# Attention and expert layer: closing the table of exponent banks, and moving four small operations on a head's maxima one place later

## The reference, cut to what matters

```python
xn = layernorm(x)                                   # x: 2 x 2048 x 256
q, k, v = split(xn @ w_qkv.T)                       # 16 heads of 16 columns
q, k = rope(q), rope(k)
attn = softmax(q @ k.T / 4)                         # per batch and head, 2048 x 2048
s = (attn @ v) @ w_out.T
e = argmax(xn @ gate_w.T)                           # one of 8 experts per token
f = (relu(xn @ wg[e])**2 * (xn @ wu[e])) @ wd[e]
out = x + s * silu(f)
```

## Time and profile before

| | us |
|---|---|
| Three runs: median (lowest to highest) | 1486.63 (1484.91 to 1490.43) |
| The profiled execution: its own time | 1485.04 |
| Its span, from the first to the last instruction | 1483.3 |
| PE busy in the span | 1450.7 (98%) |
| DVE busy | 1346.4 (91%) |
| ACT busy | 1192.4 (80%) |
| Mean granted TensorE clock | 0.998 of full |

### The profile page before, as it was taken

The page is one execution under the profiler, slowest core; times in us unless marked ns, Lnnn a source line. Parts: engine busy times, 40 slices in busy tenths (PEclk is TensorE's granted clock), DMA queues, the critical chain, the costliest instruction groups (busy, mean ns, idle before and its releaser), DMA issues.

```text
span 1483.3 us, 31996 instructions
## 1 busy us (share of the span) xinstructions
PE 1450.7 (98%) x11197; PEld 652.2 (44%) x11197; DVE 1346.4 (91%) x1979; ACT 1192.4 (80%) x2381; POOL 162.1 (11%) x221
## 2 busy tenths in 40 slices
PE   7999999999999999999999999999999999999988
PEld 5555444434475433343434344434444444434326
DVE  6689999999846999999999999999999999999906
ACT  3653588888867888888888888888888888888890
POOL 5433322200001222000010000000010000000110
PEclk9999999999999999999999999999999999999999
DMA  5875244436263455333332342333323433333323
GB/s 186 277 204 137 65 84 83 76 46 125 39 188 90 80 111 99 52 48 48 48 44 41 48 99 42 46 46 48 48 44 45 97 48 41 48 48 48 69 70 117
DMA packets 79801, 119.55 MB, mean 81 GB/s; under 512 B 28962, under 2 KB 66210, under 8 KB 72738
## 3 DMA queue, kind: packets, MB, share of 16 engines
q1 hardware_dynamic: 73714, 105.82, 36.0%
q0 software_dynamic: 3072, 8.39, 2.2%
q10 hardware_dynamic: 2896, 3.62, 0.7%
HBM read 77.15 MB, written 39.71 MB: 79 GB/s over the span
## 4 chain that ended last, share of the span: by engine, by line
PE 94%; ACT 3%; DVE 1%; issue 1%; DMA 1%; SPq 0%; POOL 0%; ACTq 0%; POOLq 0%
PE ps L1243 39%; PE ps L1257 36%; PE ps L1231 5%; PE ps L1159 3%; ACT arena L658 2%; PE ps L1437 2%; PE ps L1160 1%; PE ps L1390 1%; PE ps L1374 1%; PE ps L1192 1%; PE ps L1184 1%; PE ps L1171 1%; PE ps L1341 1%; ACT x_sb L658 1%; PE ps L1136 0%
## 5 line engine op out<-in xcount | busy, mean ns | idle before, releaser
L1231 PE MATMUL ps<-ks,qs 48*128 48x512 f32 x1984 | 692.7, 444 | 0.0
L1243 PE MATMUL ps<-qs,ks 50*128 50x512 f32 x2048 | 680.6, 435 | 9.3 <-ACT x_sb L658 7.6
L809 DVE TENSOR_REDUCE arena<-ps 128x1 f32<-128x512 f32 x992 | 639.0, 681 | 16.5 <-PE ps L1231 16.2
L658 ACT ACTIVATE arena<-ps 128x512 f32<-128x512 f32 x1056 | 564.3, 605 | 86.9 <-PE ps L1243 79.7
L812 DVE TENSOR_REDUCE arena<-ps 128x1 f32<-128x1024 f32 x496 | 603.7, 1217 | 0.8 <-PE ps L1231 0.7
L658 ACT ACTIVATE x_sb<-ps 128x512 f32<-128x512 f32 x992 | 535.3, 598 | 64.9 <-PE ps L1243 44.9
L1243 PEld LDWEIGHTS ps<-qs,ks 50*128 50x128 f32 x2048 | 329.5, 184 | 485.0 <-issue 200.9
L1231 PEld LDWEIGHTS ps<-ks,qs 48*128 48x128 f32 x1984 | 325.2, 184 | 16.5 <-DVE arena L809 9.3
L1257 PE MATMUL ps<-arena 128*32 128x256 f32 (+1 forms) x3104 | 308.5, 469 | 5.5 <-ACT arena L658 4.1
L1257 PE MATMUL ps<-x_sb,arena 128*32 128x256 f32 (+1 forms) x2960 | 290.2, 464 | 0.0
L1257 PEld LDWEIGHTS ps<-arena 128*32 128x32 f32 x3104 | 62.3, 108 | 125.6 <-issue 125.6
(11 more groups left out here) (116 smaller groups left out, 623.2 us busy)
## 6 DMA issues: line engine op xcount, KB each, us to landing
qs<-parts_d SPq DMA_DIRECT2D x186, 128.0 KB
ks<-parts_d SPq DMA_DIRECT2D x186, 128.0 KB
parts_d<-arena SPq DMA_DIRECT2D x64, 256.0 KB, 2.8
xs_d<-arena SPq DMA_DIRECT2D x13, 384.0 KB, 3.5
arena<-xs_d SPq DMA_DIRECT2D x13, 384.0 KB, 3.8
ys_d<-arena SPq DMA_DIRECT2D x13, 384.0 KB, 2.8
x_sb<-in_x SPq DMA_DIRECT2D x2, 2048.0 KB, 13.1
onum_d<-arena SPq DMA_DIRECT2D x124, 32.0 KB
```

The lines of the kernel that those rows point to most:

```text
L658: nc.scalar.activation(prob_of(pi, s, kb)[:, c * W:(c + 1) * W], ps[:, bank, :], ACT.Exp, scale=SCALE).then_inc(exp_done[bank], 1)
L809: nc.vector.tensor_reduce(most[head_slot][:, tile, u:u + 1], ps[:, AB + lo, :], AX.X, ALU.max).then_inc(a_reduced[u], 1)
L1231: ins = nc.tensor.matmul(ps[:, AB + c, :], qs[head_slot][ABASE:ABASE + KR, tile * P:(tile + 1) * P].bitcast(F32R), ks[head_slot][ABASE:ABA ...
L1243: nc.tensor.matmul(ps[:, bank, :], ks[s][at:at + KS, kb * P:(kb + 1) * P].bitcast(F32R), qs[s][at:at + KS, c * W:(c + 1) * W].bitcast(F32R ...
```

## The change

It does two things. The table gets a second bend, at place 89. The swapped order that place 25 brings is turned back there, and the table ends 0 1 2 before it starts 0 1 2 again. An assertion says so. And each k of `cut_maxima` is one place later: a step has two places for these operations, behind u = 0 and behind u = 2. The formula gives k = 0 at kb = 10, u = 2 before the change, and at kb = 11, u = 0 after it. So k = 0, 1, 2, 3 stood at (10, 2), (11, 0), (11, 2), (12, 0), and then stand at (11, 0), (11, 2), (12, 0), (12, 2).

```diff
-        BENDS = (25,)
+        BENDS = (25, 89)
...
         BANKS = banks_of_pair()
+        assert BANKS[:NBB] == [BANKS[(n - NBB) % len(BANKS)] for n in range(NBB)]
...
                     if not last_pair or (s == 0 and ahead < KB):
                         reduce(g + AHEAD, (s + 1 + ahead // KB) % 2, ahead % KB, u)
-                    k = 2 * (ahead - KB) + u // 2 + 1
+                    k = 2 * (ahead - KB) + u // 2
                     if u != 1 and 0 <= k < CUTS and coming:
                         cut_maxima(k, pi * 2 + (s + 1), 1 - s, s, (pi + 1) * 64)
```

## The result

The changed kernel took 1490.76 us in the median (1490.21 to 1491.95, 6 runs), against 1484.87 for the kernel before, measured beside it (1484.17 to 1490.43, 6 runs). The ratio is 1.0034 with a 95% interval of 1.0019 to 1.0050, so the change made the kernel 2.8 to 7.4 us slower. The forecast was 1492.3 us, in a range of 1485 to 1500. The profiled execution has a span of 1489.1 us, 5.8 more than before.

The account below looks back on a forecast made before the run. The prediction took DVE, slower than PE by 0.08 us per two steps, to set the pace. It summed +21.3 - 8.7 - 6.9 = +5.7 us, forecasting 1492.3 us after adding 1.6 for the runs' median, range 1485 to 1500.

Parts of the forecast that it names:

- DVE sets the pace: DVE's back-to-back reductions take 4.65 us per two steps against PE's 4.57, so each DVE instruction counts in full.
- The saving on DVE alone: Reduction of the maxima no longer waits for the reduction right ahead: 0.23 us at 30 heads, 6.9 us gained.
- The rival that PE could not follow: The 0.23 us per head come back as waits for PE: 6.9 us more, 1499.2 us; chance 0.09.
- The wrap: Where pairs meet, place 0 waits for place 126's exponential; closing the table saves DVE 0.62 us 14 times, 8.7 us.
- The new bend: Place 89 repeats place 25 in the other head, behind a 1.0 us product with the values; costed at nothing.
- The shift becomes the late one: B score 0 waits for the later shift transfers: DVE loses 0.76 us at 28 heads, 21.3 us.
- The 0.95 us of slack: Before the change, the last shift lands at 4.05 us behind the transposition, 0.95 us before B score 0 at 5.00.
- 0.4 were named as a sign: Sign in the changed kernel's timeline: a pair takes 0.4 us more than before.
- A transfer's time: Fourth shift transfer, from issue to landing: taken as 1.8 us, between bounds of 1.45 and 1.9.
- The rival with 2.2 us: Shift landing takes 2.2 us, making the wait 1.16 us: 11.2 us more, 1503.5 us; chance 0.05.
- The sum: Whole kernel: shift wait +21.3, wrap -8.7, DVE's own wait -6.9, giving +5.7 us.

Follow-up runs that it names:

- `close_k`: Kernel before with bends at 25 and 89 and the first three operations behind u = 0, 1, 2 of step 11, transposition unmoved: 1467.9 us, ratio 0.9882.
- `bend_80`: Kernel before with the second bend at place 80 instead of 89, the four operations unmoved: 1483.9 us, ratio 1.0001.
- `table_only`: Kernel before with the second bend at place 89 only, the four operations unmoved: 1474.8 us, ratio 0.9932.
- `no_bends`: Kernel before with no bend at all, the four operations unmoved: 1484.8 us, ratio 1.0008.
- `last_12_1b`: `close_k` with only the transposition moved one reduction later, behind u = 1 of kb = 12: 1467.7 us, ratio 0.9903 to the kernel before.
- `last_13_0`: Changed kernel with only the transposition one place later, behind u = 0 of kb = 13: 1562.7 us, ratio 1.0495 to the kernel before.
- `last_12_2b`: `close_k` with only the transposition moved two reductions later, behind u = 2 of kb = 12: 1491.8 us, ratio 1.0067 to the kernel before.
- `move_only`: Kernel before with its own table (bend at 25 alone), the four operations moved as in the change: 1494.3 us, ratio 1.0069.
- `two_more_b`: `close_k` with two more small transfers to memory issued ahead of the four shift transfers: 1471.4 us, ratio 0.9926 to the kernel before.

## Why the prediction was right

**DVE sets the pace.** Right. The saving on DVE alone came back in full in `close_k`: 0.22 us a head against 0.23 forecast. The rival that PE could not follow is out. The Trainium skill (VectorE: DVE Perf Modes, "The DRAIN you can't avoid") says that a semaphore between chained operations costs nothing extra. This case does not bear it out: with one reduction put between the operation and the one it waits for, the head got 0.22 us shorter, and the medians differ by 6.9 us.

**The wrap.** Forecast 14 x 0.62 = 8.7 us, measured 14 x 0.63 = 8.8 by the heads and 9.7 by the medians. The new bend costs nothing, and `bend_80` shows that this hangs on the place: at place 80 it cost what it saved.

**The shift becomes the late one.** Right to its sizes. The landing and the release were put at 4.10 us behind the transposition, and 4.10 was measured. DVE's loss per head was put at 0.76 and is 0.75 where it was read above. By the heads it is 38.50 - 37.70 = 0.80, and the border read above has one of the shorter gaps (0.67 us, where they lie between 0.66 and 0.73 from 685 us on). The forecast had one landing time for all heads; at heads 1, 4, 9 and 10 it was some 0.35 us later, and what made it so is not known. A pair takes 0.54 us more than before, where 0.4 were named as a sign. The 0.95 us of slack that the forecast gave the kernel before is borne out from both sides: 0.60 and 0.84 later cost nothing, 1.03 to 1.11 later costs 0.07 to 0.25, and 1.73 costs 0.78.

**A transfer's time.** From the fourth issue (919.2) to B score 0 (921.08) it is 1.9 us with the release. The value taken was 1.8 and 0.05 for the release. The rival with 2.2 us, worth 11.2 us, did not come. The Trainium skill (DMA: Bandwidth & Descriptors, "Anatomy of one DMA") gives about 2.0 us as the fixed cost of a transfer that GpSimd issues. These are issued by SyncE, and their 1.9 us is near it and a little less.

**The sum.** By the heads, +28 x 0.80 - 8.8 - 6.6 = +7.0 us. The spans differ by 5.8 and the medians by 5.9, and 5.7 was forecast. That it fits to 0.2 us is partly luck: the shift's part came out 1.1 us larger. From the transposition of head 1 to that of head 30, without the interval that holds the experts, the change costs 7.8 us in the two traces (1072.96 and 1080.73). The later landings are part of this. Against it stands the restart behind the experts (460 to 470 us of the trace), where the kernel before ran part of the stretch at the lower clock in its profiled execution. Its row, with the columns as above:

```profile
460.00:470.00 10.00, 10.00 (x62) 3.56 (x61) 5.94 (x9) 7.56 (x16) 1.36 (x2) 0.83 0.74 111
```

In the changed kernel the same stretch has a granted clock of 1.00. The interval between transpositions that holds the experts is 2.2 us shorter there (101.04 to 98.84). `table_only`, whose clock held too, takes 99.10, so about 1.9 of the 2.2 us are the clock's. The traces of `no_bends`, `close_k`, `last_12_1b` and `last_13_0` have a fall between 450 and 480 us as well, and those of the change and of the six other kernels do not. Kernels with and without the closed table, and with an early and a late transposition, stand on both sides, so nothing here ties it to the change.

The time itself was put at 1492.3 and measured at 1490.8. Nearly all of this comes from the level of the kernel before, which the forecast took as 1486.6 from three runs, and which is 1484.9 in the six runs beside the change.

**What the prediction did not see.** The forecast took a wait's price to be its length. The change leaves waits of 0.8 us, at which the clock held, and is one reduction away from waits of 1.4 us, at which it mostly did not. In `last_12_2b`, one wait of 1.36 us (head 9) was followed by such a fall, and that head took 40.57 us where the change took 38.78. The runs of `move_only` and `last_12_2b` that took 1499 us, with the change's waits, had a granted clock of 0.992 and 0.994. So the clock fell in them; at which waits it fell is not known, since neither execution was profiled.

## What to carry to other kernels

When small operations are moved to save the engine's own wait, follow what they release: here 0.22 us a head was saved on DVE and 0.80 paid behind a transfer's landing. Measure the slack of the last operation in a chain separately from the places of the others. Here three of the four could be moved for a gain and the fourth by one reduction at no cost. Two waits that end at the same instruction don't add, so a fix of the shorter is worth nothing until the longer is gone. The closed table is worth 9.7 us alone and about nothing under the late shift. And a chain that names one engine for 88% of the time does not show that this engine sets the pace; a small saving on the other one does.

## What the runs showed of the hardware

Waits of TensorE of about 1.4 us, once in 40 us, brought the granted clock from 2.4 to 1.2 GHz behind three of four in `last_13_0`, and cost 55 us on top of the 17 that the waits themselves cost over the change. The waits of 0.8 us in the profiled execution of the change and its four of 1.10 to 1.14 us did not. Four products of 128 columns, done into a bank that was to be overwritten, kept the granted clock at 0.998. SyncE took 0.65 us per issue for a transfer of 4 KB into two partitions of the on-chip stack, and 0.43 us for one of the same size to memory (`two_more_b`).
